# Layers of a two-stage state-space kernel: scans over two tiles and drives and products over four

## What is computed

```python
x  = L0_attn_x                                   # (16, 256, 128)
xn = layernorm(x);  x = x + attention(xn) * silu(mixture_of_experts(xn))
xn = layernorm(x)
h = xn
for i in range(2):                               # two Mamba layers: the stretch that the change touches
    xi, z = split(rmsnorm(h) @ in_w.T)           # 2 x 256 channels
    u = silu(causal_conv4(xi) + b)
    delta = softplus(u @ xp.T @ dt_w.T + dt_b);  B, C = u @ xp_bc.T        # 16 states
    s[l] = exp(delta[l] * A) * s[l-1] + delta[l] * B[l] * u[l]             # 256 channels x 16 states
    y = sum_n(s * C) + D_p * u
    h = (y * silu(z)) @ out_w.T + h
out = x + h * silu(coupling_net(xn))             # coupling_net: a "net", three cycles
```

## Time and profile before

| | |
|---|---|
| median of 3 runs | 2508.86 us (2505.62 to 2515.23) |
| span of the profiled execution, first to last instruction | 2311.0 us |
| the profiled execution's own time | not given apart; the median run stands 197.9 us above the span |
| the layers' scans in the span | about 1427 to 2308 us |
| busy over the span | PE 84%, DVE 71%, POOL 65%, ACT 57% |
| mean granted TensorE clock | 0.888 |

### The profile page before, as it was taken

The page is one execution under the profiler, slowest core; times in us unless marked ns, Lnnn a source line. Parts: engine busy times, 40 slices in busy tenths (PEclk is TensorE's granted clock), DMA queues, the critical chain, the costliest instruction groups (busy, mean ns, idle before and its releaser), DMA issues. The chain is left out here.

```text
span 2311.0 us, 29708 instructions
## 1 busy us (share of the span) xinstructions
PE 1940.2 (84%) x8440; PEld 871.8 (38%) x8440; DVE 1648.3 (71%) x3485; ACT 1311.8 (57%) x2685; POOL 1499.3 (65%) x1476
## 2 busy tenths in 40 slices
PE   4676499999998998886777688889899889899986
PEld 2343266665655555553333232222222222222221
DVE  4877165664656666566477324999999898999998
ACT  3354154554535455354588556776676676776663
POOL 0388485774355745408652004999999999999997
PEclk9778799999999999998788798898898898888885
DMA  9931387786765755631110004555555555555552
GB/s 379 393 94 58 89 243 216 226 236 194 198 200 166 223 162 160 186 115 50 43 36 20 0 6 110 115 115 117 118 124 120 120 128 129 130 129 126 124 123 45
DMA packets 210968, 321.50 MB, mean 139 GB/s; under 512 B 28914, under 2 KB 102644, under 8 KB 210420
## 3 DMA queue, kind: packets, MB, share of 16 engines
q1 hardware_dynamic: 194420, 286.02, 45.6%
q0 software_dynamic: 16384, 33.59, 5.1%
HBM read 207.29 MB, written 112.20 MB: 138 GB/s over the span
## 5 line engine op out<-in xcount | busy, mean ns | idle before, releaser
L1498 DVE TENSOR_TENSOR_SCAN db<-pa,db 128x512 f32<-128x512 f32 x512 | 596.5, 1205 | 50.4 <-POOL db L1549 33.8
L1549 POOL TENSOR_TENSOR db<-dur,bb 128x1024 f32<-128x1024 f32 x256 | 596.7, 2360 | 45.6 <-DMA dur<-d_scratch 44.3
L1479 ACT ACTIVATE pa<-dlr,an 128x510 f32<-128x510 f32 x512 | 339.8, 681 | 188.8 <-DVE db L1498 188.1
L1022 POOL DMA_INDIRECT yg<-y_disp,idx x256 | 255.5, 998 | 182.7 <-DMA y_disp<-yb 86.5
L725 POOL DMA_INDIRECT x_disp<-xt,idx x256 | 254.4, 994 | 147.8 <-DVE p L699 91.9
L860 ACT ACTIVATE pr<-sm,nbi 128x128 f32<-128x128 f32 (+1 forms) x512 | 228.1, 447 | 205.9 <-DVE nbi L883 204.2
L907 POOL TENSOR_SCALAR pr<-pr,rcp 128x128 f32<-128x128 f32 x320 | 135.9, 435 | 236.0 <-DVE rcp L892 233.7
L1404 PE MATMUL pb<-db,rw_all 128*32 128x512 f32 x1024 | 213.2, 703 | 81.1 <-DVE db L1504 45.4
L883 DVE CUSTOM_DVE_ANT_0 sm<-pa,rw_front 128x128 f32<-128x128 f32 (+1 forms) x512 | 160.9, 351 | 101.1 <-PE pa L780 100.8
L143 ACT ACT_TABLE_LOAD x146 | 187.3, 1283 | 55.8 <-DVE lg L587 16.2
L790 PE MATMUL pb<-rw_all,pr 128*128 128x128 f32 x768 | 144.5, 300 | 75.0 <-DVE ptt L877 47.8
(11 more groups left out here) (292 smaller groups left out, 3374.7 us busy)
## 6 DMA issues: line engine op xcount, KB each, us to landing
wb<-in_wexp SPq DMA_DIRECT2D x576, 96.0 KB
x_disp<-yb SPq DMA_DIRECT2D x8, 4608.0 KB, 30.1
xb<-x_disp SPq DMA_DIRECT2D x144, 256.0 KB
y_disp<-yb SPq DMA_DIRECT2D x144, 256.0 KB
dlr<-d_scratch SPq DMA_DIRECT2D x128, 256.0 KB, 5.2
dur<-d_scratch SPq DMA_DIRECT2D x128, 256.0 KB, 8.2
bb<-bc_scratch SPq DMA_DIRECT2D x64, 256.0 KB
d_scratch<-dl SPq DMA_DIRECT2D x32, 256.0 KB, 4.7
```

Source lines behind the costliest of these rows:

```text
L1022: e.e.indirect_dma_start(out=YG[:, t % 2, j, :], out_offset=None, in_=YD[h], in_offset=bass.IndirectOffsetOnAxis(ap=IDX[:, c:c + 1], axis= ...
L1479: e.e.activation(decay(a).rearrange("p (b l) -> p b l", b=2)[:, :, 1:256], DLR[:, h % 2, i % 4, :].rearrange("p (b l) -> p b l", b=2)[:, : ...
L1498: e.e.tensor_tensor_scan(hk(a), decay(a), hk(a), 0.0, ALU.mult, ALU.add).then_inc(s_scan, 1)
L1549: e.e.tensor_tensor(DB[:, b % ND, :, :], DUR[:, h % 2, 2 * (b % 2):2 * (b % 2) + 2, :], BB[:, b // 2 % 4, :].rearrange("p (o l) -> p o l", ...
```

## The change

The tiles stay as they are. A scan takes two tiles at once (128x1024), with their decays in two neighbouring banks; four banks hold two pairs. A drive and a product take four tiles (128x2048). C has one bank, MB. The late net uses PB[1] in place of PB[0], and waits for the second layernorm of all groups, which used that bank. The thresholds on drives that SP waits for name the same tiles in the new units.

```diff
- 'l_c': -2.4568,
- 'l_y': [4.4386, 6.8066],
+ 'l_c': 3.6,
+ 'l_y': [6.8, 6.9],
- 'l_pc': 1.5235,
+ 'l_pc': 3.5,
...
+        PD = [ctx.enter_context(nc.psum_tensor(f"pa{i}", [128, 1024], f32)) for i in range(2)]
+        PA = [PD[0][:, 0:512], PD[0][:, 512:1024], PD[1][:, 0:512]]
+        PB = [PD[1][:, 512:1024], ctx.enter_context(nc.psum_tensor("pb1", [128, 512], f32))]
...
-            return ((FB, MB), (PB[0], MB))[h][j % 2]
+            return ((FB, MB), (PB[1], MB))[h][j % 2]
...
+                            if h:
+                                e.wait_ge(s_lln, 2 * NG)
...
         def decay(a):
-            return (PA[0], PA[1], PA[2])[a % 3][:, :]
+            return PD[a // 2 % 2][:, 512 * (a % 2):512 * (a % 2) + 512]
...
         def pe_c(e):
-                    e.wait_ge(s_cm, 2 * (i - 1))
+                    e.wait_ge(s_cm, i)
-                    e.e.matmul(cb(i), SELC[:, q, :], ...
+                    e.e.matmul(CT[:, :], SELC[:, q, :], ...
         def pe_y(e):
+                        e.wait_ge(s_gm, NG)
                         e.e.matmul(YB2[:, :], DIAG[:, of_stage(s)[1], k, :], U[:, s % 2, k, :],
                                    start=True, stop=False).then_inc(s_yd, 1)
+                    multiplied(e, h, q)
                     for j in range(4):
                         a = 16 * h + 4 * q + j
-                        multiplied(e, h, 2 * q + j // 2)
         def act_scan(e):
-                    e.wait_ge(s_scan, a - 2)
+                    e.wait_ge(s_scan, a // 2 - 1)
         def dve_scan(e):
+                    b, n = 16 * s + i // 2, 8 * s + i // 4 - 1
+                    if s < NST and i < 32 and i % 2 == 0:
+                        e.wait_ge(s_dr, b // 2 + 1)
+                        e.wait_ge(s_da, 2 * b + 2)
+                        e.e.tensor_tensor_scan(pair(b), PD[b % 2][:, :], pair(b), 0.0, ALU.mult, ALU.add).then_inc(s_scan, 1)
+                    if s < NST and i > 0 and i % 4 == 0 and n % 4 != QP:
+                        c = c_tile(n // 4, n % 4)
+                        e.wait_ge(s_scan, 2 * n + 2)
+                        e.wait_ge(s_c, c + 1)
+                        e.e.tensor_tensor(four(n), four(n), each(CT[:, :]), ALU.mult).then_inc(s_cm, 1)
         def pool_scan(e):
+                for i in range(8):
+                    n, h, q = 8 * s + i, 2 * s + i // 4, i % 4
+                    yield at_scan(s, 4 * i + PL["l_dr"])
+                    if n >= ND // 2:
+                        e.wait_ge(s_ys, n - ND // 2 + 1)
+                    e.e.tensor_tensor(four(n), DUR[:, h % 2, :, :], each(BB[:, q, :]), ALU.mult).then_inc(s_dr, 1)
         def pool_c(e):
+                    n = 8 * s + 4 * k + QP
+                    yield at_scan(s, 4 * (4 * k + QP) + PL["l_pc"])
+                    e.wait_ge(s_cbi, 16 * (s + 1))
+                    e.wait_ge(s_scan, 2 * n + 2)
+                    e.e.tensor_tensor(four(n), four(n), each(CB[:, :]), ALU.mult).then_inc(s_cp, 1)
```

More of the change, by code:

```diff
@@ L259, in build @@
         SCR = nc.dram_tensor("bc_scratch", (2, 32 * N), f32, kind="Internal").ap()
-        PA = [ctx.enter_context(nc.psum_tensor(f"pa{i}", [128, 512], f32)) for i in range(3)]
-        PB = [ctx.enter_context(nc.psum_tensor(f"pb{i}", [128, 512], f32)) for i in range(2)]
+        PD = [ctx.enter_context(nc.psum_tensor(f"pa{i}", [128, 1024], f32)) for i in range(2)]
+        PA = [PD[0][:, 0:512], PD[0][:, 512:1024], PD[1][:, 0:512]]
+        PB = [PD[1][:, 512:1024], ctx.enter_context(nc.psum_tensor("pb1", [128, 512], f32))]
         PO = ctx.enter_context(nc.psum_tensor("po", [128, 512], f32))
@@ L1295, in hk, with pair, four, each @@
             return DB[:, a // 2 % ND, a % 2, :]
+        def pair(b):
+            return DB[:, b % ND, :, :].rearrange("p a l -> p (a l)")
+        def four(n):
+            return DB[:, 2 * (n % (ND // 2)):2 * (n % (ND // 2)) + 2, :, :].rearrange("p b a l -> p (b a) l")
+        def each(a):
+            return a.rearrange("p (o l) -> p o l", o=1).to_broadcast([128, 4, N])
         def decay(a):
-            return (PA[0], PA[1], PA[2])[a % 3][:, :]
+            return PD[a // 2 % 2][:, 512 * (a % 2):512 * (a % 2) + 512]
         YB2 = PB[1]
[L1303 to L1312, removed]
+        CT = MB
         def c_tile(h, q):
             return 3 * h + (q if q < QP else q - 1)
+        def multiplied(e, h, q):
+            if q == QP:
+                e.wait_ge(s_cp, h + 1)
+            else:
+                e.wait_ge(s_cm, c_tile(h, q) + 1)
         def pe_pre(e):
@@ L1385, in pe_c @@
                     e.wait_ge(s_bf, h // 2 + 1)
-                    e.wait_ge(s_cm, 2 * (i - 1))
+                    e.wait_ge(s_cm, i)
                     if h == 0:
                         e.wait_ge(s_gm, NG)
-                    e.e.matmul(cb(i), SELC[:, q, :], BCF[:, h // 2 % 2, :], start=True, stop=True).then_inc(s_c, 1)
+                    e.e.matmul(CT[:, :], SELC[:, q, :], BCF[:, h // 2 % 2, :], start=True, stop=True).then_inc(s_c, 1)
         def pe_y(e):
@@ L1486, in dve_scan @@
             e.e.memset(HN[:, :, 0:3], 0.0).then_inc(s_zero, 1)
-            for i in range(3):
-                m = e.e.memset(PA[i][:, :].rearrange("p (b l) -> p b l", b=2)[:, :, 0:1], 0.0)
+            for i in range(2):
+                m = e.e.memset(PD[i][:, :].rearrange("p (b l) -> p b l", b=4)[:, :, 0:1], 0.0)
             m.then_inc(s_zero, 1)
@@ L1492, in dve_scan @@
                 for i in range(33):
-                    a = 32 * s + i
+                    b, n = 16 * s + i // 2, 8 * s + i // 4 - 1
                     yield at_scan(s, i)
[L1495 to L1501, removed]
+                    if s < NST and i < 32 and i % 2 == 0:
[5 more added lines that the diff above has]
+                        e.wait_ge(s_scan, 2 * n + 2)
                         e.wait_ge(s_c, c + 1)
-                        db = DB[:, (a // 2 - 1) % ND, :, :]
-                        e.e.tensor_tensor(db, db, cb(c).rearrange("p (o l) -> p o l", o=1).to_broadcast([128, 2, N]),
-                                          ALU.mult).then_inc(s_cm, 1)
+                        e.e.tensor_tensor(four(n), four(n), each(CT[:, :]), ALU.mult).then_inc(s_cm, 1)
                     yield at_scan(s, i + 0.1)
@@ L1540, in pool_scan @@
             for s in range(NST):
-                for i in range(16):
-                    b, h = 16 * s + i, 2 * s + i // 8
-                    yield at_scan(s, 2 * i + PL["l_dr"])
+                for i in range(8):
+                    n, h, q = 8 * s + i, 2 * s + i // 4, i % 4
+                    yield at_scan(s, 4 * i + PL["l_dr"])
                     e.wait_ge(s_gm, NG)
                     e.wait_ge(s_dur[h % 2], 64 * (h // 2 + 1))
[L1546 to L1551, removed]
+                    e.wait_ge(s_bb[q], 16 * (s + 1))
+                    if n >= ND // 2:
+                        e.wait_ge(s_ys, n - ND // 2 + 1)
+                    e.e.tensor_tensor(four(n), DUR[:, h % 2, :, :], each(BB[:, q, :]), ALU.mult).then_inc(s_dr, 1)
         def pool_c(e):
@@ L1580, in sp_b @@
                 e.wait_ge(s_bf, s + 1)
-                e.wait_ge(s_dr, 16 * (s - 1))
+                e.wait_ge(s_dr, 8 * (s - 1))
                 e.e.dma_start(scr, BCF[:, s % 2, :]).then_inc(s_bw, 16)
@@ L1585, in sp_b @@
                     e.wait_ge(s_bw, 16 * (s + 1))
-                    e.wait_ge(s_dr, 16 * s - 8 + 2 * q + 2)
+                    e.wait_ge(s_dr, 8 * s - 3 + q)
                     e.e.dma_start(BB[:, q, :],
@@ L1595, in sp_c @@
                 e.wait_ge(s_bw, 16 * (s + 1))
-                e.wait_ge(s_cp, 4 * s)
+                e.wait_ge(s_cp, 2 * s)
                 e.wait_ge(s_gm, NG)
@@ L1609, in sp_d @@
                     e.wait_ge(s_du, 2 * s + k + 1)
-                    e.wait_ge(s_dr, 16 * (s - 1) + 8 * k)
+                    e.wait_ge(s_dr, 8 * (s - 1) + 4 * k)
                     e.e.dma_start(SD[s % 2, 1, k, :, :], DU[:, k, :]).then_inc(s_sdu[k], 16)
@@ L1624, in sp_r @@
                     e.wait_ge(s_sdu[k], 16 * (s + 1))
-                    e.wait_ge(s_dr, 8 * (h - 1))
+                    e.wait_ge(s_dr, 4 * (h - 1))
                     for n in range(4):
```

## The result

The changed kernel takes 2769.6 us in the median (2763.9 to 2773.0, 4 runs) against 2512.1 of before: ratio 1.1011, 95% interval 1.0978 to 1.1044, 257.6 us slower. The forecast was 2683 us and slower; the sign was right, the size too small, and the time lies outside the range of 2565 to 2755. Two of the kernels under Experiments, C early and the three lists in order, had one execution each some 40 to 50 us longer than their others, and their medians leave it out.

What follows compares the result with a forecast made beforehand. POOL plus a DMA loop was taken as the bound, 55.1 us per stage. The walked stage of 66.4 gave 15 x (66.4 - 55.1) = 170, plus 4: +174 on 2508.9, 2683 us, range 2565 to 2755.

Steps and rivals of the forecast that it cites:

- The bound before: Unchanged kernel's layers: a chain through POOL and a DMA loop, hardly touching DVE, sets 55.1 us per stage.
- the DMA loop of 38 us: From du of half 0 done on POOL, through du, dl and both reloads, to the next drive: 38.0 us.
- The prices of the instructions: Wider instructions: merged scan 2.20 us and product 2.18 on DVE, 128x2048 operation 4.52 on POOL.
- The prize of at most 19 us: Whole gain from fewer instructions if nothing waited longer: 1.2 us per stage x 15.5.
- The walk: One changed stage timed through all engines: 50.2 us of DVE work plus 16.2 waiting, 66.4 in all; chance 0.60.
- (c): Decays on ACT freed by pairs: table switches split pairs, so DVE's pairs 2 and 4 wait; 5.2 us across one switch.
- Rival 4: PE at 1.2 GHz in new gaps and two-bank scans of 2.41 us: 6 to 8 us more per stage, 2775 to 2805; chance 0.10.
- the base of 55.1: Unchanged stage length in us, from 14 stages between landings of half 1, subtracted from the walked stage.
- The 4 us for the last stage: Last stage, with no pre beside it: later product of quad 6 and what follows, and the coarser start, about 4 us.
- The rule weighed: Skill page: larger operations help saturated engines, smaller ones where others wait; its price gave 21 to 44 us for 352 fewer.

Runs made afterwards that it cites:

- C early: Changed kernel with C of a quad planned at 2.5 instead of 3.6, ahead of the sums of quads 2 and 6 and ds0: 2714.3 us, ratio 1.0770.
- the three lists in order: Changed kernel with C and the sums planned earlier and both decays of a pair planned at one time, widths kept: 2611.7 us, ratio 1.0414.
- POOL's fours alone: Kernel before with only POOL's drives and products over 128x2048 at the changed planned times: 2568.0 us, ratio 1.0248.
- du early: Kernel before with du of half 0 planned ahead of pair drive 12 instead of behind it: 2494.4 us, ratio 0.9948.
- the reordered kernel with POOL in twos: Changed kernel with C and sums earlier, a pair's decays together, and POOL's drives and products again over 128x1024: ratio 1.0211.

## Why the prediction was right and wrong

**The bound before**: right, though a narrow one. POOL's 17.7 us and the DMA loop of 38 us made the stage; POOL's fours alone lengthened it by 4.4 where 4.1 was worked out, and cost 61 us. du early took 2.3 us of POOL's work out of the loop and gave only 12.7 us in all.

**The prices of the instructions**: right to 0.1 us. The prize of at most 19 us for fewer instructions was never the issue.

**The walk**: right in mechanism and order. Every wait it named is in the trace; what stood behind C, ds0, ln, u0 and product 6 stood there. (c) was right as a place of waits, but in the change its cause at pair 2 is the late u and not the split pair.

**What failed** is a term of the walk: PE's durations behind its waits were taken from rows at its full clock: sum 6 by its row, bc as in its group, xi 3.7, and "ds0 59.0 to 63.0 (3.6 at full clock; at half of it up to twice that, 7.2; taken near the row, as PE has just worked)". PE had worked 1.06 us between two waits of 2.98 and 1.74 us, and ds0 took 6.1; sum 6 took 1.9, xi0 6.1, bc 3.6. Together they made product 3 end 5.3 us later per stage, 15 x 5.3 = 80 us, and with PE kept busy 4.4 of the 5.3 came back. The trace of before had these cases. The 3.70 of the earlier trace rows is xi1 of its stage; xi0 of the same stage took 5.50, and 3.9 to 5.6 in the stages around it, and ds0 began at half speed in a third of them:

```profile
1949.85 2.08 PE L1364 MATMUL pm<-dl,rw_all 128*128 128x512 f32 x2
...
2028.15 5.50 PE L1334 MATMUL pm<-hn,inc 128*128 128x512 f32 x8
```

Rival 4 named this cause and had 0.10. Of its two causes only this one came (a scan over two banks took 2.28 us, not 2.41), and 2769.6 lies just under its 2775 to 2805; the lower level had to be a part of the walk. The Trainium skill, TensorE: Matmul & The Clock Gate, Part 1: The HAM clock gate, has the array at 1.2 GHz when idle, one of two levels. The rows agree that there are two: a pair of 128x512 matmuls takes 2.04 us at one and 1.02 at the other.

A small term pulled the same way: the base of 55.1 was 0.7 too long, so that 11 us over 15 stages were missing. 174 + 80 + 11 = 265 against 257.6 measured; the 7 us between were not traced. The 4 us for the last stage are shown by no run.

**The rule weighed**: the page that the prediction cites from the Trainium skill, Perfetto Trace Analysis, Optimizing Scalar/DVE Operations, has two halves, for saturated engines and for engines that make others wait. The measurement is on the side of the second: DVE and POOL were 94% busy, yet no list had slack for pieces twice as long, and the change saved some 20 us of busy time on each and cost 258. POOL's narrow pieces back gave 42 us. But width is not most of it: with all pieces as wide, the order that puts C and the sums ahead gave 153.

## What to carry to other kernels

Before merging instructions in a pipeline of several engines, compare the fixed cost saved (0.05 us on DVE, 0.12 on POOL here) with the handover it lengthens, by a whole piece per engine and stage, and look up what the new order puts in front of each producer of a small, urgent result. Then order the lists anew for the wider pieces; here that was worth 153 of the 258 us. Walk one stage with the in-order lists: it found the waits here, and their times to a tenth until PE had idled. In such a walk, take PE behind every new gap at its lower level as the upper bound, and look for rows of the same passage behind a gap before taking one at full clock.

## What the runs showed of the hardware

- Idle matmuls ahead of waits, 12 per stage, made the changed kernel 57 us faster (granted clock 0.76 to 0.90 in the stages). In the reordered kernel with POOL in twos, 8 per stage raised it from 0.90 to 0.91 and gave 5 us, within the noise.
- A passage of PE behind a wait can cost up to double: xi 6.13 us against 3.70, bc 3.56 against 1.90, ds 6.1 against 3.5. It is not so behind each: a sum took 1.06 us after 2.98 us of idling.
- A scan over 1024 columns in two neighbouring PSUM banks takes 2.28 us, 2.20 back to back, against 1.205 for 512: crossing the bank costs nothing that shows.
- The front of the kernel takes about 190 us more on some chips, in waits of PE ("issue", up to 37 us each) and DVE ("remote") that nothing in the profile releases. Its cause was not looked into.
